# An equivariant graph network on one core: unit vectors made once, and the order of VectorE's work in one node layer

## The reference, cut to what matters

```python
src_s, src_v, dst_s, dst_v = linear maps of layernorm(x)          # per node
ms, mv = src_s[src] + dst_s[dst], src_v[src] + dst_v[dst]         # per edge
w = silu(ln(silu(ln(e @ rw1)) @ rw2)) @ rw3 + roff                # two layer norms per edge
rhat = edge_vec * rsqrt(sum(edge_vec ** 2, -1) + 1e-12)           # unit vector of an edge
Y1 = sqrt(3) * rhat
ds, dv = products of w, ms, mv with Y1 (dot, outer, cross)
alpha, vs, vv = linear maps of ds, dv
a = softmax over the edges of a destination of (leaky(alpha) . alpha_dot)
x = x + proj(segment_sum(a * (vs, vv))); x = x + feed_forward(layernorm(x)); x = layernorm(x)
```

```python
y = x @ sc * attr + gate * segment_sum(...)     # "combine"
x = layernorm(y + x)
```

## Time and profile before

| | |
|---|---|
| time, median of 3 runs | 8783.5 us (8773.5 to 8791.46) |
| the profiled execution: its own time | 8718.24 us |
| its span | 8716.4 us |
| VectorE / GpSimd busy over the span | 71% / 58% |
| TensorE matmul / weight load busy | 75% / 67% |
| stages (by the joins and the load of the engines) | setup to 95, node_pre to 650, edge_logits 650 to 1960, edge_softmax to 2590, node_first to 3980, edge layer 1 to 4780, node layer 1 to 5430, edge layer 2 to 6270, node layer 2 to 7080, edge layer 3 to 8050, node layer 3 to 8710 us |

### The profile page before, as it was taken

One profiled execution on the slowest core, in us unless ns is written; L12 is line 12 of the kernel. 1 busy time (PEld: TensorE's weight loads), 2 busy tenths in 40 slices (PEclk: granted clock), 3 DMA queues, 4 the chain that ended last, 5 costly groups with the idle time before them and its releaser, 6 DMA issues. The chain is left out here.

```text
span 8716.4 us, 182003 instructions
## 1 busy us (share of the span) xinstructions
PE 6567.3 (75%) x41992; PEld 5838.5 (67%) x41992; DVE 6227.6 (71%) x20668; ACT 4108.6 (47%) x9608; POOL 5093.1 (58%) x4620
## 2 busy tenths in 40 slices
PE   3667777774557888888998666899865679999555
PEld 3455666664447777777888666788755569998554
DVE  4667888885548888885665667566588877775787
ACT  1334555552224444444444667444366654444444
POOL 4668888884435444444554777555466644443777
PEclk9887888885559999999999888899978889999665
DMA  6872333337873333333444566445455544443555
GB/s 133 182 173 79 89 89 88 90 85 145 164 155 92 99 96 99 99 98 102 125 126 114 181 190 192 120 123 125 110 169 166 170 129 120 119 120 106 154 162 155
DMA packets 910393, 1118.45 MB, mean 128 GB/s; under 512 B 458518, under 2 KB 546422, under 8 KB 910032
## 3 DMA queue, kind: packets, MB, share of 16 engines
q1 hardware_dynamic: 728032, 812.69, 33.4%
q0 software_dynamic: 182144, 303.64, 14.7%
HBM read 650.35 MB, written 465.65 MB: 128 GB/s over the span
## 5 line engine op out<-in xcount | busy, mean ns | idle before, releaser
L451 POOL DMA_INDIRECT erow<-e_rows,edge_idx x1176 | 1247.3, 1061 | 1229.6 <-issue 1137.3
L671 POOL DMA_INDIRECT agg<-seg_rows,edge_idx x1568 | 1554.3, 991 | 656.4 <-issue 483.2
L720 POOL TENSOR_TENSOR stats<-stats,power 128x8 f32<-128x8 f32 (+1 forms) x588 | 751.8, 1279 | 866.1 <-DVE xo L712 444.4
L400 PE MATMUL banks<-w_all,xt 128*128 128x128 f32 (+1 forms) x2352 | 546.2, 369 | 795.7 <-DVE y_more L945 259.5
L400 PEld LDWEIGHTS banks<-w_all,xt 128*128 128x128 f32 x2352 | 429.3, 248 | 879.8 <-issue 872.2
L486 PEld LDWEIGHTS banks<-seg,mid 128*128 128x128 f32 x7840 | 931.9, 194 | 15.1
L486 PE MATMUL banks<-seg,mid 128*128 128x128 f32 x7840 | 933.4, 277 | 0.0
L534 ACT ACTIVATE mid_t<-banks 128x512 f32<-128x512 f32 x980 | 585.1, 597 | 315.3 <-PE banks L486 311.7
L403 PE MATMUL banks<-w_all,xt 128*128 128x128 f32 x3528 | 657.7, 339 | 0.0
L403 PEld LDWEIGHTS banks<-w_all,xt 128*128 128x128 f32 x3528 | 617.5, 254 | 0.0
L498 PE MATMUL banks<-w_all,mid_t 128*128 128x161 f32 (+1 forms) x2352 | 583.9, 330 | 2.8 <-ACT res L539 2.8
(11 more groups left out here) (276 smaller groups left out, 18225.2 us busy)
## 6 DMA issues: line engine op xcount, KB each, us to landing
x_rows<-xo SPq DMA_DIRECT2D x294, 324.0 KB, 2.6
xin<-x_rows SPq DMA_DIRECT2D x294, 324.0 KB
e_rows<-ets SPq DMA_DIRECT2D x294, 322.0 KB
dst_row<-in_dst_flat SPq DMA_DIRECT2D x294, 256.0 KB
xin<-in_x SPq DMA_DIRECT2D x196, 324.0 KB, 7.1
seg_rows<-res SPq DMA_DIRECT2D x196, 322.0 KB, 2.6
seg_rows<-res SPq DMA_DIRECT2D x98, 384.0 KB, 2.3
seg_rows<-res SPq DMA_DIRECT2D x98, 338.0 KB, 6.6
```

What stands on the lines that cost most here:

```text
L400: pe.matmul(flat[:, to + k * cols:to + (k + 1) * cols], of[:, k * P:(k + 1) * P], W(w_s), start=True, stop=True)
L451: pool.indirect_dma_start(erow[s.quad][:, t, 0:EROW], None, table, bass.IndirectOffsetOnAxis(idx[s.slot][:, t:t + 1], 0),).then_inc(rows_i ...
L671: pool.indirect_dma_start(agg[s.quad][:, t, 0:SUM_COLS[layer]], None, seg_rows[layer], bass.IndirectOffsetOnAxis(idx[s.slot][:, t:t + 1], ...
L720: pool.tensor_tensor(st[:, at + n:at + 2 * n], st[:, at:at + n], power[:, 0:n], ALU.pow) \
```

## The change

1. The setup stage loads the edge vectors of all 50,176 edges into one tile of 128 x 2352 (`vec`), and computes squared lengths, square root (ScalarE), reciprocal with one correction step, and the products, nine VectorE operations in all; the result is stored to `unit_dram`. The input `vec` is laid out on the host so that a partition's numbers lie together.
2. In `edge_logits` the length part of `var2`, the `unit` product in `ln2` and their waits are gone; the power takes 8 columns. The unit vectors are loaded from `unit_dram` into four buffers that hold a chunk until `leaky` has used it. The load stands behind the index load in SyncE's queue and waits for `leaky` of four chunks before; `message` waits for the load.
3. In node layer 1 VectorE's round is `combine(t-1)`, `final_bias(t-2)`, `before(t)`. Layer 2 keeps the old order; layer 3 had the new one.

```diff
-                    if with_e:
+                    if layer == 2:
                         pipeline(dve, chunks, [(before, 0), (lambda s: final_bias(dve, s), 2), (combine, 1)])
                     else:
                         pipeline(dve, chunks, [(combine, 1), (lambda s: final_bias(dve, s), 2), (before, 0)])
...
-                unit = [sb(f"unit_{k}", [P, TILES, 6], own=own) for k in range(4)]
+                unit = attr
...
                     def load_vectors(s):
-                        sp.wait_ge(ln2_step.sem, ln2_step.after((s.g - 3) * 2))
-                        sp.wait_ge(var2_step.sem, var2_step.after((s.g - 1) * 4))
-                        sp.dma_start(attr[s.quad][:], inp["vec"][bass.ds(s.g * CHUNK, CHUNK), :]
-                                     .rearrange("(t p) c -> p t c", p=P)).then_inc(attr_in[s.slot].sem, 16)
+                        sp.wait_ge(leaky_step.sem, leaky_step.after((s.g - 3) * leaky_steps))
+                        sp.dma_start(unit[s.quad][:].rearrange("p t c -> p (t c)"), unit_dram[:, bass.ds(s.g * 6 * TILES, 6 * TILES)]) \
+                            .then_inc(units_quad[s.quad].sem, 16)
...
-                    pipeline(sp, chunks, [(load_scalars, 0), (load_vectors, 1), (load_indices, 2), (load_penalties, 6),
+                    pipeline(sp, chunks, [(load_scalars, 0), (load_indices, 2), (load_vectors, 3), (load_penalties, 6),
...
-                        roots(s, 32 if both else 36, 44)
+                        roots(s, 32 if both else 36, 40)
...
                     def var2(s):
-                        dve.wait_ge(attr_in[s.slot].sem, attr_in[s.slot].after(s.half + 1))
-                        a = chain.did(dve.tensor_tensor(vec_sq[s.slot][:], v, v, ALU.mult).then_inc(chain.sem, 1))
-                        chain.did(dve.tensor_scalar(st[:, 36:40], psum[:, 5, VAR:VAR + 4], 1e-5, None, ALU.add).then_inc(chain.sem, 1))
-                        dve.wait_ge(chain.sem, chain.after(a))
-                        a = chain.did(dve.tensor_reduce(st[:, 56:60], vec_sq[s.slot][:], AX_X, ALU.add).then_inc(chain.sem, 1))
-                        dve.wait_ge(chain.sem, chain.after(a))
-                        chain.did(dve.tensor_scalar(st[:, 40:44], st[:, 56:60], 1e-12, None, ALU.add).then_inc(chain.sem, 1))
+                        dve.tensor_scalar(stats[s.slot][:, 36:40], psum[:, 5, VAR:VAR + 4], 1e-5, None, ALU.add).then_inc(var2_step.sem, 1)
...
-                        chain.did(dve.tensor_tensor(
-                            unit[s.quad][:, :, 1:6], attr[s.quad][:, :, 1:6],
-                            spread(stats[s.slot][:, 52:56], 2, [P, TILES, 5]), ALU.mult).then_inc(chain.sem, 1))
...
-                        dve.wait_ge(ln2_step.sem, ln2_step.after((s.g + 1) * 2))
+                        dve.wait_ge(units_quad[s.quad].sem, units_quad[s.quad].after(s.quarter + 1))
...
+                    sp.dma_start(vec[:], inp["vec"]).then_inc(units_in.sem, 16)
...
+                    sp.wait_ge(setup_step.sem, setup_step.after(units_after))
+                    sp.dma_start(unit_dram, vec[:].rearrange("p t c -> p (t c)")).then_inc(setup_out.sem, 16)
...
+                    act.wait_ge(setup_step.sem, setup_step.after(stores_after + 3))
+                    act.activation(error[:], length[:], ACT.Sqrt).then_inc(length_sb.sem, 1)
...
+                    dve.wait_ge(units_in.sem, units_in.after(1))
+                    k = chain.did(dve.tensor_tensor(vec_sq[:], vec[:, :, 1:4], vec[:, :, 1:4], ALU.mult).then_inc(chain.sem, 1))
+                    k = chain.did(dve.tensor_reduce(length[:], vec_sq[:], AX_X, ALU.add).then_inc(chain.sem, 1))
+                    k = chain.did(dve.tensor_scalar(length[:], length[:], 1e-12, None, ALU.add).then_inc(chain.sem, 1))
+                    dve.wait_ge(length_sb.sem, length_sb.after(1))
+                    k = chain.did(dve.reciprocal(inverse[:], error[:]).then_inc(chain.sem, 1))
+                    k = chain.did(dve.tensor_tensor(error[:], inverse[:], inverse[:], ALU.mult).then_inc(chain.sem, 1))
+                    k = chain.did(dve.tensor_tensor(error[:], error[:], length[:], ALU.mult).then_inc(chain.sem, 1))
+                    k = chain.did(dve.tensor_scalar(error[:], error[:], -0.5, 1.5, ALU.mult, ALU.add).then_inc(chain.sem, 1))
+                    k = chain.did(dve.tensor_tensor(inverse[:], inverse[:], error[:], ALU.mult).then_inc(chain.sem, 1))
+                    assert chain.did(dve.tensor_tensor(vec[:, :, 1:], vec[:, :, 1:], spread(inverse[:], 2, [P, tiles, 5]), ALU.mult)
+                                     .then_inc(chain.sem, 1)) == units_after
```

73 lines of the change are left out of this document (38 added, 35 removed).

## The result

The changed kernel takes 8659.3 us (median of 4 runs, 8643.8 to 8662.7) against 8779.5 us before (median of 4, 8773.5 to 8791.5). The ratio is 0.9858, with a 95% interval of 0.9841 to 0.9875: 110 to 140 us faster. The forecast was 93 us, which this interval leaves out. The direction and the two places were right, and the gain was larger than forecast: 8659.3 us lies only 4 us above the lower end of the range of 8655 to 8752.

A forecast was written before the change was run, and what follows sets the result against it. It took GpSimd's own work to bound the logits and a two-round loop through GpSimd, the gather's landing and VectorE to bound node layer 1. -53 - 52 + 12 = -93 us, 8783.5 to 8690; range 8655 to 8752.

The forecast's parts named there:

- the narrower power: Logits: GpSimd's power over 8 columns instead of 12 takes 1.714 us instead of 2.391, 0.68 us less per round.
- the cut loop of node layer 1: Node layer 1: with combine first, the 14.07 us loop spans three rounds instead of two, 4.7 us per round instead of 7.0.
- neither TensorE's clock nor an index load takes over: Logits and node layer 1: clock stays near today's; node layer 1's index load has 4.8 us left for 2 KB.
- signs of being wrong: A granted clock well below 0.8 in either stage, GpSimd waiting for an index load, or logits gathers longer than today's.
- node layer 1, "-52 us": Combine first: 6.42 us per round instead of 6.96, 0.54 less over 96 rounds; bounds 69 us and zero.
- The Trainium skill's rule: Node layer 1: two-SBUF-input VectorE operations and GpSimd SBUF reads lock each other out; rows agree to 0.18 us per power.
- The logits, "-53 us": Logits: the narrower power gains 0.55 us in each of 96 rounds; 65 us if GpSimd stays the bound, lower end 29.
- the cap of 0.55 us per round at TensorE: Logits: of TensorE's 1.08 us wait per round 0.52 is handing over, so 0.56 can go before TensorE sets the pace.
- rival D: Both stages: gathers lengthen as the power shortens, or waits only change names; only setup's +12 us remains, 8795 us; chance 0.06.
- "Four VectorE operations less: nothing": Logits: at most 0.68 us per round less VectorE work, but VectorE is not the bound, so no gain by itself.
- The setup, "+12 us": Setup: added VectorE chain and square root with table load sum to 11.8 us; late vector load 0 to 5 us more.
- The difference between profile and median: Whole kernel: sums used the profiled 8718.2 us; the median of 8783.5 lies 65.3 us above, assumed the same after the change.

The follow-up runs named there:

- e1: The kernel before the change, unchanged, run and profiled again on chip B: 9102.5 us, ratio 1.0016.
- e10: The changed kernel with node layer 1's old VectorE order and each power of that layer issued twice: 8723.9 us, ratio 0.9992 to the kernel before.
- e16: The changed kernel with every power of node layer 1 issued twice on GpSimd, on chip E: 8973.4 us, ratio 0.9937 to the kernel before.
- e8: The changed kernel with every power of node layer 1 issued twice on GpSimd, on chip C: 9091.2 us, ratio 0.9950 to the kernel before.
- e9: The changed kernel with four VectorE operations on an idle tile added to each logits round, on chip D: 8624.1 us, ratio 0.9882 to the kernel before.
- e7: The changed kernel with vectors loaded first and unit vectors computed first in the setup, on chip C: 9027.5 us, ratio 0.9881 to the kernel before.
- e12: The changed kernel with combine first and later gates in node layer 2, plus unit vectors made early in setup: 8632.7 us, ratio 0.9887 to the kernel before.
- e15: The changed kernel with the unit vectors made early in the setup, on chip E: 8884.8 us, ratio 0.9849 to the kernel before.

## Why the prediction came out as it did

**The direction and the places were right.** Four of its steps have their rows: the narrower power (1.72 us), the cut loop of node layer 1, the added chain in the setup, and that neither TensorE's clock nor an index load takes over. One of its own signs of being wrong came all the same: the gathers of the logits are longer than before, by 0.10 us per round.

**The mis-sized term is node layer 1, "-52 us".** It measured -69 on A and -65 in both comparisons with e1 on B. Three things made it too small. The power beside `combine` was priced at 1.22 us after node layer 3 and took 1.10, so the round is 6.33 us and not 6.42; that is 9 us. The stage has 98 rounds, not 96: 1 us. And the stage is longer than 98 steady rounds, by 26 us before (708.3 - 98 x 6.96) and by 19 us after (638.9 - 98 x 6.33): the start and the end gained 7 us that a count of steady rounds does not see. The total landed on the prediction's upper bound of 69 us, but by another sum: the steady rounds make 62 of it, the start and the end 7. The mechanism is shown: a second power cost half its length in the old order (e10), and no wait stood before either power in the new one (e16, e8).

The Trainium skill's rule (page "SBUF — State Buffer", section "SBUF: two separate sides") holds here in sign and is small in size: the power takes 1.12 us on A and 1.19 on E beside a VectorE operation of that kind against 1.04 without (read behind e16). Four more operations with two SBUF inputs, for which GpSimd hardly waits, cost 15 of their 20 us through longer instructions of GpSimd (e9).

**The logits, "-53 us", came out at -54.8 for another reason than given.** I had put the cap of 0.55 us per round at TensorE, whose spare time would be used up. TensorE still waits 0.66 us per round and GpSimd is still the bound. Of the 0.669 us that the power gave, 0.10 went back into longer gathers (8.70 us for eight against 8.61) and 0.05 into waiting. That was the first half of rival D, at a seventh of the size. "Four VectorE operations less: nothing" was a term put at nothing by the wait that they cause; by e9 it is worth up to 20 us, since GpSimd's own instructions lengthen beside them. So that the number fits is luck: the power (65 us) and the four operations (20) would be 85 us, and some 30 us were lost to something that no run isolates; the gathers, which should have become shorter by 0.1 us a round, became longer by 0.1.

**The setup, "+12 us", was +14:** 10.7 us of chain, where 11.8 had been worked out with a table load of 1.28 us that ran 64 us ahead of it, and 3.3 us of later loads inside the 0 to 5 us allowed. The reciprocal took 2.60 us and not 2.2; at 6.6 ns per column it does not go by the 5.1 of 32 columns. The price was avoidable. In e7, e12 and e15 the same chain lies under the loads and the setup takes 97.8 to 99.0 us, what is left over being the later loads.

**The difference between profile and median was carried over unchanged.** One execution doesn't bear that: the two profiles differ by 74 us and the medians by 120, and two untouched stages full of transfers moved by 36 us from the one profile to the other.

Sum with measured terms: -54.8 - 69.4 + 14.0 = -110 us, against -120 us timed with an interval of -110 to -140. Some 10 us stay unassigned, 0 to 30 by the interval.

## What to carry to other kernels

Where an engine stands still before one short instruction in every round, follow the loop that returns to it and count the rounds that it spans: cutting it is worth the difference to that engine's own work, and delaying something in it costs its length divided by the rounds. Price an instruction of VectorE also by what it does to GpSimd's instructions beside it, and not only by its wait: here four for which GpSimd hardly waited cost 20 us. Work that is made once belongs where the engine waits for loads anyway.

## What the runs showed of the hardware that was not expected

The same kernel takes 8733 us on one chip and 9141 us on another. On the slower ones ScalarE and VectorE have waits of mostly 1 to 7 us (the longest 13.4 us, in e15) that no instruction of this kernel's queues is seen to end (`ACT res L539 <- remote: 196.0, 45, 5.1` in e1, none on A), and in the round shown above TensorE's clock is at half after the gap they make; its mean over 800 to 1900 us of e1 is 0.74, where A has 0.87 over 800 to 1800. The logits take 1561 us there and 1357 on A; how much of it is waiting and how much the clock isn't separated. The change is worth 1.4% on A and 1.0 to 1.2% on B and E. In the kernel before on A an indirect gather of 128 rows took GpSimd 1.58 us (at 1244.24) and the next one 0.95, with nothing waited for.
